# Ternary feed-forward weights made by VectorE instead of GpSimd, and packed weights unpacked later

## The chip, the cores and the metric

The kernel runs on one core of one Trainium2 chip, as one launch of one program. The metric is the device time of that launch in microseconds (us), from its start to the stored output. The core has five engines that run their own instruction streams side by side and meet only at semaphores: TensorE (PE in the profile), VectorE (DVE), ScalarE (ACT), GpSimd (POOL) and SyncE (SP, which here issues every DMA).

## The reference, cut to what matters

Two perceiver layers over 128 query rows of 256 channels, each layer being cross-attention, self-attention and a feed-forward. The two feed-forwards and their weights are what the change is about:

```python
# layer 0's feed-forward: weights rounded to -1, 0, 1 by their own mean magnitude
def _quantize(W):
    gamma = jnp.mean(jnp.abs(W))
    return jnp.clip(jnp.round(W / (gamma + EPS)), -1.0, 1.0)
Wq1, Wq2 = _quantize(W1), _quantize(W2)          # 1024x256 and 256x1024
h = jax.nn.relu(jnp.einsum('bsd,fd->bsf', x, Wq1) + b1)
out = jnp.einsum('bsf,df->bsd', h, Wq2) + b2
# layer 1's feed-forward: four 2-bit weights in each int32
enc = (packed_weight[None, :] >> shifts[:, None] & 3).reshape(-1)[:n]
w = (enc.astype(jnp.float32) - 1.0).reshape(OUT_F, IN_F) * weight_scale
# order of the whole
x = x + _L0_xattn_ref(_layernorm(x), ctx_768, ...)   # 12544 keys
x = x + _L0_attn_ref(_layernorm(x), ...)
x = x + _L0_ffn_ref(_layernorm(x), ...)
x = x + _L1_xattn_ref(_layernorm(x), ctx_768, ..., mask)
x = x + _L1_attn_ref(_layernorm(x), ...)
x = x + _L1_ffn_ref(_layernorm(x), ...)
```

## The kernel before

**Stages.** Layer 0's cross-attention goes over the 12544 keys in 14 chunks of 896 and fills the first 529 us of the span. A short serial stretch follows: its output projection (x0 to x1 in the code's names), the gated self-attention, and the ternary feed-forward. Then comes layer 1's cross-attention over the keys that the mask keeps, its self-attention and its feed-forward. In the serial stretch every step waits for the one before: VectorE normalises `x`, TensorE transposes it, ScalarE copies it out of PSUM, TensorE multiplies, VectorE adds the result to `x`.

**Order.** There is no scheduler. Each engine's stream is written out by hand in its own function, and runs in that order; semaphores (the dictionary `S`) tie the streams together. What an engine has not reached yet is late, however short it is.

**A layernorm needs GpSimd.** `layernorm` (L845 to L859) computes mean and variance on VectorE (L847, L848), adds epsilon (L853, or L851 for the double one), and then asks GpSimd for the power -0.5 through the semaphore `to_power`; GpSimd does it in `power` (L443), and VectorE waits for `power` before it scales `x` into `xn` (L856). The layernorms are tagged x0, x1, x2, x3, x4 and x5. x1, x2 and x3 lie in the serial stretch, and their three calls of `power` stand in GpSimd's stream after the last chunk.

**The ternary weights.** W1 and W2 lie together in the tile `ffw` (128x4096, f32). In the last chunk VectorE sums their magnitudes (L1026), TensorE adds the partitions up (L1499), and VectorE makes of it plus and minus half of the mean, in `thr` (L1034 to L1036). GpSimd then waits for `thr` and turns `ffw` into -1, 0, 1 in four pieces of 1024 columns, with three instructions each: `w < -t` into the scratch tile `wraw` (L508), `w > t` in place (L510), and the difference (L512). The power of x1 stands after the second piece, those of x2 and x3 after the fourth. TensorE waits for all twelve steps (`tern`) before the first product of the feed-forward (L1556); `ffw` is free again when the second (L1563) has ended.

```python
for n in range(4):                                             # GpSimd, from L506
    w, k = ffw[:, 1024 * n:1024 * n + 1024], n // 2
    nc.gpsimd.tensor_scalar(wraw_flat, w, thr[:, 2 + k:3 + k], None, ALU.is_lt ...)
    nc.gpsimd.tensor_scalar(w, w, thr[:, k:k + 1], None, ALU.is_gt ...)
    nc.gpsimd.tensor_tensor(w, w, wraw_flat, ALU.subtract ...)
```

**The packed weights.** `unpack(s)` (two VectorE instructions, L1076 and L1078, on 128x128) is called four times between `thr` and the output of the first attention; its result `wtf` is read by the very last product of the kernel.

**Filling.** Where TensorE would stand idle in the serial stretch, `keep_busy(bank, n)` (L1318) issues n products with a tile of zeros whose result nobody reads. They stand in TensorE's own order, ahead of the wait for the next real operand. Other names used below: L1090 is VectorE's first step on the attention's output; L1109 spreads the logarithm of the gate over 128 columns; L730 is an exponential of ScalarE; L1306 is TensorE's transposition of `xn`; L1539 sums the gates; L1575 makes layer 1's queries; L1151 is VectorE's first step on what they give. At L378 SP waits for the end of the feed-forward (`y` at 3) and then issues the loads of layer 1's first keys.

## Time and profile before

| | us |
|---|---|
| median of 3 runs | 920.91 (920.09 to 921.3) |
| the profiled execution, its own time | 919.66 |
| span of the trace in it | 917.8 |
| TensorE busy | 857.3 |
| VectorE busy | 628.9 |
| ScalarE busy | 427.2 |
| GpSimd busy | 217.6 |

The profile is one execution; its times in the trace count from the start of the span. TensorE is busy for 93% of the span, but part of this is the filling with zeros, so its busy share alone doesn't say that it bounds a stretch. What bounds one is read from the timeline of its engines and from the chain of waits, which follows back from the last instruction what released what. A row of the timeline gives the start, the duration of the (merged) instructions, the engine, line and operation, output and inputs, and in brackets the idle time before it and what ended that.

### The profile page before, as it was taken

How to read it: one execution, taken by the hardware profiler on the slowest of the kernel's cores; microseconds unless marked ns; L12 is line 12 of the kernel's file. 1: busy time of each engine (PE TensorE's matmuls, PEld its weight loads, DVE VectorE, ACT ScalarE, POOL GpSimd, SP SyncE). 2: the span in 40 equal slices, each digit the busy share in tenths (PEclk: the TensorE clock that was granted, in tenths of full speed). 3: DMA queues.
4: the chain of work that ended last, by engine and by line, in shares of the span. 5: the costliest groups of instructions: out<-in, count | busy, mean ns of one | idle time of the engine just before them, and what ended most of it. 6: DMA issues, size and time to landing. Idle time of an engine off the chain costs nothing.

```text
span 917.8 us, 21933 instructions
## 1 busy us (share of the span) xinstructions
PE 857.3 (93%) x7662; PEld 663.3 (72%) x7662; DVE 628.9 (69%) x1104; ACT 427.2 (47%) x578; POOL 217.6 (24%) x233
## 2 busy tenths in 40 slices
PE   3889999999999999999999988998999999999798
PEld 2567777777777777777777757654688887888676
DVE  5768568568568568567567643699487878777373
ACT  2245765765765766766765721300233333333122
POOL 4182022022022022022020392350033232222000
PEclk9669999999999999999999999999999999999798
DMA  5845645645645645648635133210000000000000
GB/s 178 197 128 124 180 114 120 178 115 120 175 118 120 172 120 120 170 123 211 168 85 122 48 139 106 81 39 1 7 19 13 18 14 19 13 19 7 1 1 7
DMA packets 43867, 85.16 MB, mean 93 GB/s; under 512 B 11616, under 2 KB 26657, under 8 KB 41889
## 3 DMA queue, kind: packets, MB, share of 16 engines
q1 hardware_dynamic: 43822, 84.62, 35.9%
q8 instruction: 21, 0.34, 0.2%
q14 instruction: 24, 0.19, 0.1%
HBM read 45.03 MB, written 0.25 MB: 49 GB/s over the span
## 4 chain that ended last, share of the span: by engine, by line
PE 69%; issue 12%; DVE 10%; POOL 4%; ACT 2%; SPq 1%; DMA 1%; DVEq 0%; ACTq 0%; POOLq 0%
PE ps L1642 9%; PE ps L1455 9%; PE ps L1467 8%; PE ps L1373 8%; PE ps L1363 7%; PE ps L1356 6%; DVE cu L918 6%; PE ps L1650 5%; PE ps L1663 5%; PE ps L1643 2%; PE ps L1382 1%; PE ps L1389 1%; POOL ffw L510 1%; POOL wraw L508 1%; PE ps L1616 1%
## 5 line engine op out<-in xcount | busy, mean ns | idle before, releaser
L918 DVE TENSOR_REDUCE cu<-ps 128x1 f32<-128x448 f32 x448 | 250.4, 618 | 53.2 <-PE ps L1373 51.2
L668 ACT ACTIVATE pr<-ps 128x1024 f32<-128x1024 f32 x196 | 190.1, 1023 | 66.4 <-PE ps L1455 65.6
L435 POOL TENSOR_TENSOR pause<-pause 128x1 f32<-128x1 f32 x41 | 12.8, 314 | 569.5 <-DVE mr L930 377.5
L1373 PE MATMUL ps<-khl,qp 32*128 32x448 f32 x448 | 123.9, 483 | 2.6 <-DVE khl L908 0.8
L1455 PE MATMUL ps<-qs,ks 128*128 128x256 f32 x784 | 122.6, 296 | 3.3 <-ACT qs L627 3.1
L1455 PEld LDWEIGHTS ps<-qs,ks 128*128 128x128 f32 x784 | 101.9, 190 | 21.7 <-issue 20.6
L1467 PE MATMUL ps<-pr,v 128*17 128x128 f32 x3136 | 104.6, 274 | 0.5 <-DVE ps L995 0.5
L1642 PE MATMUL ps<-ks,ct 128*128 128x512 f32 x352 | 98.2, 400 | 0.3 <-ACT pr L788 0.3
L1467 PEld LDWEIGHTS ps<-pr,v 128*17 128x17 f32 x3136 | 77.2, 97 | 22.2 <-issue 19.1
L1373 PEld LDWEIGHTS ps<-khl,qp 32*128 32x128 f32 x448 | 57.9, 188 | 48.9 <-DVE cu L918 14.0
L908 DVE SCALAR_TENSOR_TENSOR khl<-ps,bk,khl 128x448 fp32r<-128x448 f32 x56 | 37.1, 682 | 74.5 <-ACT khl L615 74.5
L1206 DVE TENSOR_SCALAR ps<-ps 128x1024 f32<-128x1024 f32 x44 | 54.1, 1229 | 46.2 <-PE ps L1643 46.2
L788 ACT ACTIVATE pr<-ps 128x1024 f32<-128x1024 f32 x44 | 45.3, 1030 | 81.3 <-DVE ps L1206 81.3
L1642 PEld LDWEIGHTS ps<-ks,ct 128*128 128x128 f32 x352 | 64.8, 189 | 17.6 <-issue 3.4
L1363 PE MATMUL ps<-wv,ct 128*128 128x256 f32 x490 | 72.9, 298 | 4.5 <-DVE cu L918 3.6
L1363 PEld LDWEIGHTS ps<-wv,ct 128*128 128x128 f32 x490 | 65.3, 194 | 15.3 <-DVE cu L918 7.9
L1356 PE MATMUL ps<-ct,wk 128*128 128x448 f32 x280 | 68.9, 387 | 2.1 <-DVE khl L908 2.1
L621 ACT COPY v<-ps 128x256 f32<-128x256 f32 x98 | 36.6, 374 | 60.3 <-PE ps L1363 59.1
L1189 DVE TENSOR_TENSOR pr<-pr,wraw 128x1024 f32<-128x1024 f32 x45 | 55.0, 1223 | 4.0 <-issue 4.0
L1356 PEld LDWEIGHTS ps<-ct,wk 128*128 128x128 f32 x280 | 52.5, 198 | 6.4 <-DVE khl L908 2.5
L1193 DVE TENSOR_TENSOR nm<-nm,pr 128x1024 f32<-128x1024 f32 x45 | 55.4, 1232 | 1.5
L1173 DVE CUSTOM_DVE_ANT_0 pr<-ps,khl 128x1024 f32<-128x1024 f32 x48 | 55.5, 1220 | 0.0
(263 smaller groups left out, 1143.7 us busy)
## 6 DMA issues: line engine op xcount, KB each, us to landing
ks<-khl SPq DMA_DIRECT2D x168, 224.0 KB, 4.9
nm<-maxima SPq DMA_DIRECT2D x14, 1024.0 KB, 4.6
raw<-in_ctxT SPq DMA_DIRECT2D x14, 448.0 KB, 3.9
raw<-in_ctxT SPq DMA_DIRECT2D x28, 224.0 KB, 4.4
ffw<-in_mask_q SPq DMA_DIRECT2D x1, 1568.0 KB, 9.6
raw<-in_ctxT SPq DMA_DIRECT2D x12, 128.0 KB, 2.2
raw<-in_ctxT SPq DMA_DIRECT2D x22, 64.0 KB, 1.8
raw<-in_ctxT SPq DMA_DIRECT2D x44, 32.0 KB, 2.0
```

What stands on the lines that cost most here:

```text
L668: nc.scalar.activation(pr[:, (HALVES * b + u) % 4, :], bank(2 * (u % 2), 2), ACT.Exp).then_inc(S["e0_exp"], 1)
L918: V.tensor_reduce(cu2[:, h, half:half + 1], ps[:, use_bank(n), 0:NB], AX_X, ALU.max).then_inc(S["e0_red"], 1)
L1173: nc.vector.tensor_tensor_reduce(out=junk[:, h % 2], in0=ps[:, 2 * (h % 4):2 * (h % 4) + 2, :], in1=negm[:, b, :].bitcast(F32).rearrange(" ...
L1189: V.tensor_tensor(sl, sl, mk[:, u // 2, :].unsqueeze(1).to_broadcast([P, 8, T]), ALU.mult).then_inc(S["e1_masked"], 1)
L1193: V.tensor_tensor(acc, acc, pr[:, u, :], ALU.add).then_inc(S["e1_sum"], 1)
L1206: V.tensor_scalar(bank(2 * (u % 2), 2), bank(2 * (u % 2), 2), 80.0, None, ALU.min).then_inc(S["e1_ok"], 1)
L1356: last = mm(dst, wk0[:, w, t * P:(t + 1) * P], ct[:, b, xx, half * NB:(half + 1) * NB], start=(j == 0), stop=(j == 4))
L1363: last = mm(ps[:, use_bank(n), 0:C], ct[:, b, xx, t * P:(t + 1) * P], wv0[:, w, :], start=(j == 0), stop=(j == 4))
L1373: mm(ps[:, use_bank(n), 0:NB], qp[part, t, e, :], khl[part, 0, t, half * NB:(half + 1) * NB], start=True, stop=True).then_inc(S["e0_head"], 1)
L1455: last = mm(ps[:, 2 * z + k // 2, (k % 2) * 256:(k % 2) * 256 + 256], ks_v[:, b, gg, t * P:(t + 1) * P], qs[:, gg * 256:gg * 256 + 256], s ...
L1467: last = mm(ps[32 * j:32 * j + 17, 4, (h // 4) * T:(h // 4 + 1) * T], v17_v[:, b, t, h, :], pr[:, (HALVES * b + u) % 4, k * T:(k + 1) * T] ...
L1642: mm(ps[:, 2 * z + j, :], cu[:, t, xx, :], asp[:, w, cols], start=(i == 0), stop=False)
```

## The change

GpSimd's twelve instructions and its waits for `thr` and the load of the weights go; its stream goes from the last chunk's work straight to the three powers. VectorE makes the ternary weights, right behind `thr`, with two instructions for each piece: `w < -t` into `wraw`, and one `scalar_tensor_tensor` that takes `(w > t) - wraw` in place. TensorE waits for 4 steps in place of 12. The four calls of `unpack` move from the end of the last chunk to behind the double layernorm x3, ahead of VectorE's wait for layer 1's folded queries.

```diff
@@ GpSimd @@
-            pool.wait_ge(S["thr"], 1)
-            pool.wait_ge(S["ld_ffw"], 32)
             pool.wait_ge(S["e0_lo"], NCH + 1)
-            for n in range(4):
-                w, k = ffw[:, 1024 * n:1024 * n + 1024], n // 2
-                nc.gpsimd.tensor_scalar(wraw_flat, w, thr[:, 2 + k:3 + k], None, ALU.is_lt
-                                        ).then_inc(S["tern"], 1)
-                nc.gpsimd.tensor_scalar(w, w, thr[:, k:k + 1], None, ALU.is_gt).then_inc(S["tern"], 1)
-                pool.wait_ge(S["tern"], 3 * n + 2)
-                nc.gpsimd.tensor_tensor(w, w, wraw_flat, ALU.subtract).then_inc(S["tern"], 1)
-                pool.wait_ge(S["tern"], 3 * n + 3)
-                if n == 1:
-                    power(rstd[:, :], expo[:, 0:1])
-            power(rstd[:, :], expo[:, 0:1])
-            power(rstd[:, :], expo[:, 0:1])
+            for _ in range(3):
+                power(rstd[:, :], expo[:, 0:1])
@@ VectorE @@
             dve.sem_inc(S["thr"], 1)
+            for n in range(4):
+                w, k = ffw[:, 1024 * n:1024 * n + 1024], n // 2
+                link(V.tensor_scalar(wraw_flat, w, thr[:, 2 + k:3 + k], None, ALU.is_lt))
+                V.scalar_tensor_tensor(w, w, thr[:, k:k + 1], wraw_flat, ALU.is_gt, ALU.subtract).then_inc(S["tern"], 1)
+                dve.wait_ge(S["tern"], n + 1)
             dve.wait_ge(S["ld_small"], 16 * 9)
...
-            for n in range(4):
-                unpack(n)
...
             link(V.memset(ml, 0.0))
             link(V.memset(mx[:, :], -3.0e38))
+            for n in range(4):
+                unpack(n)
             total = dve.value_load(sup[0:1, 1, 0:1], min_val=0, max_val=NUNIT)
@@ TensorE @@
-            pe.wait_ge(S["tern"], 12)
+            pe.wait_ge(S["tern"], 4)
```

GpSimd's stream behind the last chunk's work, before (the tile names are those of the code; `rstd` is the layernorm's; a row's `x2` counts two in a row):

```order
L469 TENSOR_TENSOR dm<-con,mr 128x1024
L508 ISA
L508 TENSOR_SCALAR wraw<-ffw,thr 128x1024
L510 TENSOR_SCALAR ffw<-ffw,thr 128x1024
L512 TENSOR_TENSOR ffw<-ffw,wraw 128x1024
```

After, at the same place:

```order
L469 TENSOR_TENSOR dm<-con,mr 128x1024
L443 TENSOR_TENSOR rstd<-rstd,expo 128x1 x3
L508 MEMSET khl 32x256
L511 MEMSET ct 64x2x1024
L515 TENSOR_LOAD sup
```

Of the four triples before, the first is shown; the power of x1 stood behind the second, and now all three powers are next, with nothing of the weights ahead of them.

VectorE's stream behind the thresholds, before:

```order
L1036 TENSOR_SCALAR thr<-thr 128x2
L1037 TENSOR_SCALAR kept<-ps 49x1
L1040 TENSOR_SCALAR con<-con 128x128
L1041 TENSOR_SCALAR slp<-slp 128x16
L1042 TENSOR_SCALAR nbg<-nbg 128x1
L1076 TENSOR_SCALAR wq<-pk 128x128
L1078 TENSOR_SCALAR wq<-wq,fsc 128x2x64
```

After, at the same place (the first of the four pairs):

```order
L1023 TENSOR_SCALAR thr<-thr 128x2
L1024 TENSOR_SCALAR thr<-thr 128x2
L1025 TENSOR_SCALAR kept<-ps 49x1
L1029 TENSOR_SCALAR wraw<-ffw,thr 128x1024
L1030 SCALAR_TENSOR_TENSOR ffw<-ffw,thr,wraw 128x1024
```

The four pairs on 1024 columns have taken the place of the four pairs of `unpack` on 128 (`wq` is the tile under `wtf`), and stand ahead of L1040's counterpart; in both kernels the next instruction behind these is the reciprocal of the attention's output (L1090, L1079 after). In layer 1's beginning VectorE now has:

```order
L1133 MEMSET oacc 128x512
L1134 MEMSET mx 128x16
L1069 TENSOR_SCALAR wq<-pk 128x128
L1071 TENSOR_SCALAR wq<-wq,fsc 128x2x64
L1069 TENSOR_SCALAR wq<-pk 128x128
```

Four such pairs stand there, and behind them the reading of two counts and the step on the folded queries (L1142, which was L1151).

## Rows read from the trace of the kernel before

**Rows 1.** Chain of waits, 529 to 565 us: start, us, engine, output, line

```profile
537.40 2.84 POOL wraw L508
...
553.77 0.57 POOL rstd L443
554.34 0.03 issue
554.37 0.42 DVE xn L856
...
564.50 0.37 SPq L285
```

**Rows 2.** GpSimd's groups by line, 519 to 555 us: busy us, mean ns

```profile
L510 POOL TENSOR_SCALAR ffw<-ffw,thr 128x1024 f32<-128x1024 f32 x4 | 11.7, 2915 | 0.0
L508 POOL TENSOR_SCALAR wraw<-ffw,thr 128x1024 f32<-128x1024 f32 x4 | 11.5, 2868 | 19.6 <-issue 19.4
L512 POOL TENSOR_TENSOR ffw<-ffw,wraw 128x1024 f32<-128x1024 f32 x4 | 9.4, 2354 | 0.3
```

**Rows 3.** VectorE's timeline, x1 to x3: start, us, instruction, idle before it

```profile
535.05 0.15 DVE L853 TENSOR_SCALAR rstd<-mv 128x1 f32<-128x1 f32 x1
537.44 1.21 DVE L856 TENSOR_SCALAR xn<-x,mv,rstd 128x256 f32<-128x256 f32 x1 [2.23 <-POOL rstd L443]
...
543.59 1.99 DVE L1109 TENSOR_SCALAR xn<-con,g 128x128 f32<-128x128 f32 x1 [1.33 <-ACT g L728]
...
550.70 0.15 DVE L853 TENSOR_SCALAR rstd<-mv 128x1 f32<-128x1 f32 x1
...
565.72 0.15 DVE L851 TENSOR_SCALAR rstd<-mv 128x1 f32<-128x1 f32 x1
566.60 0.48 DVE L856 TENSOR_SCALAR xn<-x,mv,rstd 128x256 f32<-128x256 f32 x1 [0.72 <-POOL rstd L443]
```

**Rows 4.** Timeline of TensorE in the serial stretch

```profile
533.88 2.57 PE L1318 MATMUL ps<-zero 128*128 128x256 bf16 x22
538.76 0.44 PE L1306 MATMUL ps<-con,xn 128*128 128x128 f32 x2 [2.31 <-DVEq L862]
...
545.69 0.49 PE L1539 MATMUL ps<-con,xn 128*128 128x128 f32 x2 [1.98 <-DVEq L1110]
...
555.86 5.16 PE L1556 MATMUL ps<-xnT,ffw 128*128 128x128 f32 x32
...
568.60 3.84 PE L1575 MATMUL ps<-xnT,pr 128*128 128x128 f32 x32 [0.41 <-ACT xnT L744]
```

**Rows 5.** Windows: length, busy us of PE, PEld, DVE, ACT, POOL, then granted TensorE clock

```profile
552.00:554.90 2.90, 0.01 (x1) 0.01 (x1) 0.41 (x1) 0.00 (x0) 2.25 (x2) 1.00 0.00 0
554.90:561.00 6.10, 6.10 (x39) 5.81 (x40) 1.12 (x2) 2.26 (x3) 0.00 (x0) 0.72 0.00 0
...
868.00:872.60 4.60, 4.60 (x20) 3.52 (x19) 1.38 (x2) 0.81 (x2) 0.00 (x0) 0.65 0.00 0
```

**Rows 6.** Timeline of VectorE at the kernel's end, forms like the new ones

```profile
888.21 1.23 DVE L1257 SCALAR_TENSOR_TENSOR pr<-pr 128x1024 f32<-128x1024 f32 x1
889.47 0.69 DVE L1260 TENSOR_SCALAR pr<-pr 128x1024 f32<-128x1024 f32 x1
...
911.87 0.35 DVE L1283 TENSOR_SCALAR xn<-xn,rstd 128x256 f32<-128x256 f32 x1
912.26 0.29 DVE L1284 TENSOR_SCALAR xn<-xn 128x256 f32<-128x256 f32 x1
```

**Rows 7.** VectorE's timeline around the thresholds

```profile
519.66 0.15 DVE L1037 TENSOR_SCALAR kept<-ps 49x1 f32<-49x1 f32 x1
519.97 0.23 DVE L1040 TENSOR_SCALAR con<-con 128x128 f32<-128x128 f32 x1
...
530.42 0.26 DVE L1090 RECIPROCAL rl<-ps 128x16 f32<-128x16 f32 x1 [4.45 <-PE ps L1507]
```

**Rows 8.** Timeline of ScalarE: its exponential of the gates

```profile
546.97 0.31 ACT L730 ACTIVATE xn<-xn 128x128 f32<-128x128 f32 x1 [2.11 <-DVEq L1114]
```

**Rows 9.** Timeline of VectorE at layer 1's folded queries

```profile
580.28 2.60 DVE L1151 TENSOR_TENSOR ks<-ps,ks 128x1024 fp32r<-128x1024 f32 x2 [10.01 <-ACT ks L766]
```

## The prediction

> **What bounds the kernel now.** I read the chain of waits first, since it names what released what in the stretch that the change touches. Between the end of the last chunk and the second feed-forward product it runs almost wholly on GpSimd: one of its comparisons starts at 537.40, and its power for the layernorm x2 is done only at 554.34, after which VectorE scales x and the chain goes on to SP's loads for layer 1 at 564.50 [rows 1]. The groups of GpSimd then give the price of this work: four comparisons of 2.87 us, four of 2.92 and four subtractions of 2.35, 32.6 us in all [rows 2]. It begins once the thresholds are there, at about 520, so it can't be over before 553, and the power of x2 is queued behind it.
>
> The timeline of VectorE shows what is waited for. In x3, where GpSimd is free, the step from the start of the epsilon addition to the start of the scaling takes 566.60 - 565.72 = 0.88 us. In x1 it takes 537.44 - 535.05 = 2.39, and in x2 554.37 - 550.70 = 3.67 [rows 1, 3]. TensorE, the engine that is nearly always busy, is idle at just these places: 2.31 us before it can transpose x1, 1.98 before L1539, and for all but 0.01 of the 2.90 us from 552.0 to 554.9 [rows 4, 5]. So here a serial chain is the bound and not an engine's throughput.
>
> **The change part by part.** *The new work on VectorE.* No row shows these instructions, so they are put together from near ones. A comparison of a tensor with a per-partition scalar on 1024 columns: the tensor_scalar on 1024 columns with immediates takes 0.69, and a scalar taken from a tile adds 0.35 - 0.29 = 0.06, so 0.75 [rows 6]. The scalar_tensor_tensor: 1.23 plus the same 0.06, so 1.29 [rows 6]. Consecutive dependent instructions lie about 0.04 us apart in the timeline, and each pair has two such steps. A pair is 2.1 us, and four are 8.5. They start where L1037 has ended and been waited for, at 519.85, and end at 528.4. The three small steps L1040 to L1042 follow, of about 0.2 each with their gaps, so VectorE is through at 529.1 [rows 7]. It next has to be there at 530.42, for L1090, which waits for TensorE [rows 7]. The work is hidden with 1.3 us to spare, by the last chunk's scores, exponentials and weighing, in which VectorE has no part. Cost: 0. From below, it can't be a gain by itself. From above: if the comparison runs no faster than the two-input form, it costs 1.29 too, the pairs end at 530.5, VectorE is through at 531.2 and L1090 starts 0.8 late. I take 0, since L1260 is a row of the same operation, shape and memory.
>
> *Removed from GpSimd.* With 32.6 us gone it is idle when x1 and x2 ask for the power, as it is in x3.
>
> Term A, x1: the wait shrinks by 2.39 - 0.88 = 1.51 [rows 3]. The scaling itself took 1.21 us, with a comparison of GpSimd beside it from 537.40; the same instruction took 0.48 in x3 and 0.42 in x2, where no comparison ran [rows 1, 3]. That is 0.79 more, together 2.30. TensorE has 22 filling products ahead of the transposition, which run from 533.88 to 536.45, and the transposition started at 538.76 [rows 4]. So at most 2.31 can be had here, and the filling is just not late. Term A is 2.3.
>
> Term B, L1109: 1.99 us for 128 columns with one scalar from a tile [rows 3]. L1040 takes 0.23 for 128 columns with immediates [rows 7], plus 0.06 for the scalar is 0.29, so 1.70 goes if GpSimd's presence is the reason, as in x1. Behind it TensorE had been idle for 1.98 and ScalarE's exponential for 2.11 [rows 4, 8], both more than 1.70, so neither filling nor a table load becomes the bound. Term B is 1.7, with 0 as the other end if the length of this instruction has a cause of its own.
>
> *A rule weighed against the row.* The scaling of x1 ran from 537.44 to 538.65, and the comparison beside it from 537.40 to 540.24 [rows 1, 3]: it was held up, but was done 1.6 us before GpSimd was. The Trainium skill (SBUF — State Buffer, section "Who interferes with whom") says of such a pair that the one that issues first has the shared port for its whole instruction and "the other **fully blocks** (not throttle)". By that, the scaling would not have ended before 540.24, and term A could have been 1.6 larger before the filling capped it; by the row it is what stands above. On the direction, that VectorE gains when GpSimd leaves, rule and row agree.
>
> Term C, x2: 3.67 - 0.88 = 2.79 [rows 1, 3]. TensorE's filling doesn't reach into it, since TensorE is idle for 2.9 us before the transposition [rows 5]. Term C is 2.8.
>
> Term D, the clock. After that idle stretch the granted clock of the stretch 554.9 to 561.0 is 0.72: part of the feed-forward's first product runs at 1.2 and not at 2.4 GHz [rows 5]. Its 32 records take 5.16 us, where the 32 records of the same shape in L1575 take 3.84 [rows 4]. With terms A to C the idle stretches of 2.3, 2.0 and 3.1 us shrink to 0.0, 0.3 and 0.3, so I expect no fall here: 1.3, with 0 as the other end.
>
> *TensorE's wait for the weights.* They are ready at 528.4, and needed at about 548: nothing.
>
> *unpack, moved.* Four pairs of about 0.23 and 0.29, some 2.3 us with gaps, come before VectorE's step on the folded queries, in front of which it sat idle for 10.01 us [rows 7, 9]. It issues no DMA and nobody waits on VectorE in there. Cost 0; the cover is ScalarE's and TensorE's making of the queries and the loads of the first keys, and even if it were gone the cost would be 2.3. Taking it from its old place gains nothing, since VectorE waited there for 4.45 us [rows 7].
>
> *What is late next.* Everything behind 564.50 hangs on SP's issue after the feed-forward, and moves forward as a whole. The loads of layer 1's weights are issued at the end of the last chunk and are not in the chain.
>
> **The sum.** 2.3 + 1.7 + 2.8 + 1.3 = 8.1 us. Against the profiled execution's own 919.66 (917.8 of span and 1.9 around it) that gives 911.6. This execution lies 1.25 us under the median of the runs, so for a median I take 920.9 - 8.1 = 912.8.
>
> **The rivals.** *The clock does not follow.* Terms A to C come, but the fall of the clock stays or comes back elsewhere. For it: the trace has falls without an idle stretch before them, as at 868.0 to 872.6, where TensorE is busy for all 4.6 us at 0.65 of the clock [rows 5]. Against it: the fall at 555 comes right after the longest idle stretch of this part. The gain is then 6.8, so 914.1. The Trainium skill (TensorE: Matmul & The Clock Gate, section "What's actually happening") has the chip judge activity in a window that runs freely, so that the point of change differs between runs of one kernel; by that rule any shift of 7 us may move other falls too. How much one is worth is in the row: 0.35 of 4.6 us short of full clock is 1.6 us of work at 2.4 GHz. One more of them with the old one kept makes 915.7, one fewer with the gain of 8.1 makes 911.2.
>
> *VectorE is late for L1090.* The comparison takes 1.29: 0.8 us back, 913.6.
>
> *It was hidden anyway.* If the head of layer 1 waits for something that doesn't move, such as its loads, the gain before 564.50 is lost: 920.9. Against it: SP issues these only after the feed-forward [rows 1].
>
> *Slower.* VectorE may be no better at these comparisons than GpSimd. At 2.9 us for each of the eight, the pairs end at 519.85 + 4 x 5.9 = 543.3, VectorE is through at 544.0 and the attention's output waits 13.6 us for it, in the middle of the chain. Less A to C (6.8), the clock lost, it is 6.8 slower: 927.7. It turns where a pair costs the 2.1 that I expect plus (1.3 + 8.1) / 4 = 2.35 more, at 4.5 us. For it speaks only that no row has a comparison on VectorE; against it that its arithmetic on 1024 columns takes 0.69 to 1.23 throughout [rows 6].
>
> **How the numbers follow.** My forecast 912.8 gets 0.70; the clock that does not follow 0.16 (914.1, up to 915.7); VectorE late 0.06 (913.6); one fall fewer 0.03 (911.2); hidden anyway 0.03; slower 0.02. The range from 911.0 to 915.8 holds the first four, with term B's absence (914.5) too, and leaves out about 1 in 10. A difference under 0.2% (1.8 us) can't be told from no change in a measurement of this kernel. Faster by more: 0.95; within: 0.03; slower: 0.02.
>
> **What would show it.** Right: no GpSimd work between the last chunk and x1; 0.88 us from epsilon to scaling in x1 and x2; 0.42 for the scaling of x1 and 0.29 for L1109; pairs of 0.75 and 1.29; VectorE idle before the reciprocal; granted clock 1.00 through the first feed-forward product, and its 32 records in about 3.85. SP's first load after the feed-forward at about 556.4 in place of 564.5. Wrong: VectorE released by itself at the reciprocal, a clock under 1.00 in the feed-forward, or a gap behind 556 that was not there before.

## The result, and the profile after

| | median, us | lowest to highest |
|---|---|---|
| before, 5 runs | 920.63 | 920.09 to 921.3 |
| after, 5 runs | 907.82 | 906.85 to 913.62 |
| the profiled execution of after | 913.62 | span 911.8 |

The ratio is 0.9877, with a 95% interval from 0.9849 to 0.9905. The changed kernel is faster, by 12.8 us where 8.1 were forecast, and 907.82 lies 3.2 us below the low end of the range.

The two traces are compared first by stage. These are windows of before and then of after: from the start to the end of the second chunk (the opening); the other chunks up to the thresholds; from there to the end of the feed-forward (the serial stretch); layer 1 up to its attention's output; and the tail. A row has the window, its length, the busy time of PE, PEld, DVE, ACT and POOL, and then the granted clock of TensorE, the DMA share and GB/s. The row of the chunks is left out in both.

```profile
0.00:95.23 95.23, 72.98 (x490) 53.30 (x491) 65.54 (x115) 36.41 (x57) 38.23 (x25) 0.84 0.63 160
...
519.06:564.59 45.53, 37.93 (x391) 30.53 (x391) 19.92 (x52) 15.31 (x22) 33.58 (x14) 0.96 0.19 71
564.59:858.88 294.29, 279.87 (x1756) 214.59 (x1756) 225.06 (x299) 78.92 (x81) 74.42 (x146) 0.99 0.10 28
858.88:917.80 58.92, 52.79 (x360) 42.55 (x356) 29.00 (x60) 12.07 (x15) 1.12 (x2) 0.88 0.01 3
```

```profile
0.00:99.32 99.32, 73.44 (x490) 54.00 (x491) 66.39 (x115) 36.41 (x57) 38.03 (x25) 0.86 0.60 154
...
522.96:560.27 37.31, 36.44 (x391) 29.09 (x391) 20.08 (x51) 15.31 (x22) 1.10 (x2) 1.00 0.23 86
560.27:855.59 295.32, 280.96 (x1756) 214.86 (x1756) 226.75 (x306) 78.89 (x81) 75.02 (x146) 0.98 0.10 28
855.59:911.80 56.21, 50.02 (x360) 40.81 (x356) 29.00 (x60) 12.06 (x15) 1.13 (x2) 0.93 0.01 3
```

The serial stretch gave 45.53 - 37.31 = 8.22 us. It is the only stage whose work the change touches, apart from `unpack`. But the opening, whose instructions are the same in both kernels, took 4.09 us more, layer 1's attention 1.03 more, the chunks 0.19 less, and the tail, also the same, 2.71 less. So these two executions lie only 6.0 us apart, and 6.0 is the sum of an 8.2 that belongs to the change and of things that don't. The moved `unpack` is not behind the 1.03 (below); the clock is at 1.2 GHz there from 638.5 to 645.5 us in after (0.51 granted), and for about half as long in before (0.74 from 641.0 to 647.5). The forecast and the miss both sit in this table.

First the stretch itself. VectorE's timeline of after (start, duration, instruction, idle before it and what ended it):

```profile
523.86 0.75 DVE L1029 TENSOR_SCALAR wraw<-ffw,thr 128x1024 f32<-128x1024 f32 x1
524.65 1.28 DVE L1030 SCALAR_TENSOR_TENSOR ffw<-ffw,thr,wraw 128x1024 f32<-128x1024 f32 x1
...
530.97 1.28 DVE L1030 SCALAR_TENSOR_TENSOR ffw<-ffw,thr,wraw 128x1024 f32<-128x1024 f32 x1
...
534.25 0.26 DVE L1079 RECIPROCAL rl<-ps 128x16 f32<-128x16 f32 x1 [1.33 <-PE ps L1498]
...
538.82 0.15 DVE L841 TENSOR_SCALAR rstd<-mv 128x1 f32<-128x1 f32 x1
539.79 0.41 DVE L844 TENSOR_SCALAR xn<-x,mv,rstd 128x256 f32<-128x256 f32 x1 [0.82 <-POOL rstd L443]
...
545.15 0.29 DVE L1098 TENSOR_SCALAR xn<-con,g 128x128 f32<-128x128 f32 x1 [1.33 <-ACT g L716]
...
550.56 0.15 DVE L841 TENSOR_SCALAR rstd<-mv 128x1 f32<-128x1 f32 x1
551.44 0.41 DVE L844 TENSOR_SCALAR xn<-x,mv,rstd 128x256 f32<-128x256 f32 x1 [0.72 <-POOL rstd L443]
```

The four pairs run from 523.86 to 532.25 at 0.75 and 1.28 us each. VectorE then still waits 1.33 us for TensorE before the reciprocal, so the new work is hidden. In x1 the step from epsilon to scaling is 0.97 us and the scaling 0.41; L1098 takes 0.29; in x2 the step is 0.88. The rows that answer to them stand in [rows 3] and [rows 7].

The moved `unpack` stands in layer 1's beginning, ahead of the step on the folded queries:

```profile
575.89 2.60 DVE L1142 TENSOR_TENSOR ks<-ps,ks 128x1024 fp32r<-128x1024 f32 x2 [7.61 <-ACT ks L754]
```

VectorE still waits 7.61 us for ScalarE there (10.01 in before [rows 9]), and the step starts 15.62 us after the stretch's end, where before has 15.69. So the move cost nothing, as forecast.

TensorE's timeline of after, and behind it the window of both feed-forward products:

```profile
537.71 2.57 PE L1309 MATMUL ps<-zero 128*128 128x256 bf16 x22
540.32 0.44 PE L1297 MATMUL ps<-con,xn 128*128 128x128 f32 x2
...
545.55 0.49 PE L1530 MATMUL ps<-con,xn 128*128 128x128 f32 x2 [0.28 <-DVEq L1099]
...
551.97 0.44 PE L1297 MATMUL ps<-con,xn 128*128 128x128 f32 x2 [0.28 <-DVEq L850]
...
552.86 3.84 PE L1547 MATMUL ps<-xnT,ffw 128*128 128x128 f32 x32
```

```profile
552.86:559.99 7.13, 7.13 (x48) 6.63 (x49) 2.57 (x5) 1.84 (x2) 0.00 (x0) 1.00 0.00 0
```

The third idle stretch of before, ahead of x2's transposition, has this row in its timeline of TensorE:

```profile
554.89 0.44 PE L1306 MATMUL ps<-con,xn 128*128 128x128 f32 x2 [3.07 <-DVEq L862]
```

Of the three idle stretches of before (2.31 and 1.98 us [rows 4], and this 3.07) 0, 0.28 and 0.28 are left. The granted clock is 1.00, the level of 2.4 GHz, through both products, and the 32 matmuls take 3.84 us in place of 5.16.

Then the opening. The rows of VectorE and GpSimd in the timeline of before, in order of time:

```profile
13.58 2.63 DVE L893 TENSOR_TENSOR v<-xn,con 128x256 f32<-128x256 f32 x2
13.86 2.08 POOL L457 TENSOR_TENSOR ct<-raw,ct 128x896 fp32r<-128x896 f32 x1 [9.29 <-issue]
...
16.25 2.18 DVE L895 CAST qp<-v 128x512 fp32r<-128x512 f32 x1
...
18.21 6.23 POOL L476 MEMSET ks<- 32x7168 f32 x1
...
19.30 5.17 DVE L901 TENSOR_SCALAR mr<-mx 128x16 fp32r<-128x16 f32 x1
```

And of after, with TensorE's first product behind it:

```profile
13.53 2.07 POOL L457 TENSOR_TENSOR ct<-raw,ct 128x896 fp32r<-128x896 f32 x1 [9.13 <-issue]
13.87 4.22 DVE L881 TENSOR_TENSOR v<-xn,con 128x256 f32<-128x256 f32 x2
...
17.87 6.07 POOL L476 MEMSET ks<- 32x7168 f32 x1
18.13 6.09 DVE L883 CAST qp<-v 128x512 fp32r<-128x512 f32 x1
...
25.26 0.58 PE L1467 MATMUL ps<-zero 128*128 128x512 bf16 x1 [12.07 <-DVEq L885]
```

An instruction of VectorE on 16 columns takes 5.17 us in before: it ends at 24.47, just as GpSimd's memset does at 24.44. In after the memset holds the cast instead: 6.09 us, where the same cast takes 0.43 in `gpsimd_busy` (below), with GpSimd idle beside it. The cast's 2.18 in before is not its own length either, since GpSimd's second subtraction (64x896, from 16.01 to 18.14) runs beside it. The cast stands ahead of TensorE's first product, so TensorE stands for 12.07 us behind it; in before and in `after_ordered` (below) it is 6.58.

The order is made one step earlier. In after GpSimd's first subtraction, on 128x896, starts 0.34 us ahead of VectorE's two products into `v`, and these take 4.22 us; in before it starts 0.28 us behind them, and they take 2.63. Nothing in the program orders these two, so a few tenths of a microsecond decide which instruction is caught. The Trainium skill (SBUF — State Buffer, "Who interferes with whom") has for such pairs the engine that issues first hold the shared port for its whole instruction while the other is blocked; at the memset the traces agree. At x1's scaling they don't: that ended 1.6 us before the comparison beside it [rows 1, 3], as the prediction had it.

### The profile page after: what moved, and what is told of

It is laid out like the page before. It is cut to its first block, busy times and chain, and to the rows that moved or that the text cites. A ratio compares the mean times of both kernels' runs of the same rounds, so it can differ in the third digit from the quotient of the medians.

```text
span 911.8 us, 21931 instructions
## 1 busy us (share of the span) xinstructions
PE 854.5 (94%) x7662; PEld 661.0 (72%) x7662; DVE 631.6 (69%) x1112; ACT 427.1 (47%) x578; POOL 185.5 (20%) x221
## 4 chain that ended last, share of the span: by engine, by line
PE 73%; DVE 11%; issue 11%; ACT 2%; SPq 1%; DMA 1%; DVEq 0%; POOL 0%; ACTq 0%; POOLq 0%
PE ps L1446 10%; PE ps L1633 9%; PE ps L1458 9%; PE ps L1364 8%; PE ps L1354 7%; PE ps L1347 7%; DVE cu L906 6%; PE ps L1641 6%; PE ps L1654 5%; PE ps L1634 2%; PE ps L1373 1%; PE ps L1380 1%; PE ps L1607 1%; PE ps L1309 1%; PE ps L1609 1%
## 5 line engine op out<-in xcount | busy, mean ns | idle before, releaser
L896 DVE SCALAR_TENSOR_TENSOR khl<-ps,bk,khl 128x448 fp32r<-128x448 f32 x56 | 37.3, 684 | 77.2 <-ACT khl L603 77.2
## 6 DMA issues: line engine op xcount, KB each, us to landing
ks<-khl SPq DMA_DIRECT2D x168, 224.0 KB, 5.0
raw<-in_ctxT SPq DMA_DIRECT2D x28, 224.0 KB, 4.3
```

## The experiments

Each kernel ran beside runs of before on the same chip; medians are compared within one session, and kernels of different sessions by their ratios to before. A ratio comes with its 95% interval, and isn't exactly that of the two medians. The expectations on record stand with each. For the stages I use the same five bounds as above; "the stretch" is the serial one.

### The changed kernel again, and both kernels with the opening's order fixed

`after_again` has no edit. `after_ordered` and `before_ordered` are the two kernels with one wait more, which holds GpSimd's first memset of `ks` back until VectorE is through with the opening's steps:

```diff
+            pool.wait_ge(S["v_ones"], 2)
             nc.gpsimd.memset(ks[96:P, 0:GROUPS * CH].bitcast(F32), 1.0)
```

> The changed kernel once more, unaltered. In its first profile the unchanged opening of the kernel was 3.9 us longer than before's (thresholds at 522.96 and not 519.06), while the serial stretch from there to the end of the first feed-forward was 8.2 us shorter (37.31 against 45.53). Theory: the opening can go two ways, according to whether GpSimd's memset of ks (6 us) gets in ahead of VectorE's cast to qp. Where it does, a run takes 912 to 914; where not, 907 to 910. Then the serial stretch is 37.3 +- 0.3 in this profile too, whatever the opening does. Rival: the opening is fixed by the program and the spread comes from TensorE's clock in layer 1; then the thresholds are at 523.0 +- 0.3 again, and the times differ behind the feed-forward.

> The changed kernel, in which GpSimd's first memset of ks waits until VectorE is through with its opening (semaphore v_ones at 2), so that it can't hold up the cast to qp. Theory of the opening: the cast takes 0.4 to 2.2 us and not 6.1, the thresholds come at 519.0 or earlier, and the runs lie together within 1.5 us at 905 to 908. Rival (clock in layer 1): the times still spread over 4 us or more.

> The kernel before, with the same wait in the opening and nothing of the change. It gives the change its value with the opening out of the way. Theory: 917 to 920, and the changed kernel with the same wait is 8 to 10 us faster (8.2 of the serial stretch, the rest from falls of the clock that are met or missed). Rival: the median gain of 12.8 us is all the change's; then the two differ by 12 to 13.5.

| | median, us | runs, lowest to highest | ratio to before | opening | stretch | tail |
|---|---|---|---|---|---|---|
| before, same session | 919.84 | 25, 911.72 to 922.26 | | | | |
| after_again | 910.84 | 8, 909.1 to 914.14 | 0.9922 (0.9892 to 0.9951) | 97.18 | 37.32 | 56.10 |
| after_ordered | 907.59 | 6, 904.48 to 908.81 | 0.9881 (0.9847 to 0.9915) | 92.21 | 37.33 | 59.10 |
| before_ordered | 913.46 | 12, 911.16 to 916.66 | 0.9951 (0.9928 to 0.9975) | 90.59 | 45.32 | 56.69 |

VectorE and GpSimd in the opening of `after_ordered`:

```profile
14.61 2.18 DVE L884 CAST qp<-v 128x512 fp32r<-128x512 f32 x1
16.82 2.44 DVE L885 TENSOR_TENSOR dm<-v,qp 128x512 fp32r<-128x512 f32 x1
19.41 0.17 DVE L890 TENSOR_SCALAR mr<-mx 128x16 fp32r<-128x16 f32 x1
...
20.22 6.07 POOL L477 MEMSET ks<- 32x7168 f32 x1 [1.51 <-DVE v L892]
```

The same instruction on 16 columns takes 0.17 us when the memset is not beside it, and the openings are 95.23 - 90.59 = 4.6 us shorter than in the trace of before above, and 99.32 - 92.21 = 7.1 shorter than in that of after. It holds in every trace: the seven kernels with this wait and no filling in the first chunk (those of this and the next three sections) have openings of 90.59 to 92.21 us, the nine traces without it 93.77 to 99.32. The wait orders only the memset, though: the steps before it still meet GpSimd's two subtractions, here the cast (2.18 for 0.43) and VectorE's own subtraction behind it (2.44 for 0.69, its time in before).

In medians the one wait is worth 919.84 - 913.46 = 6.4 us in before and 910.84 - 907.59 = 3.3 in after. In means of the same runs it is 919.05 - 913.74 = 5.3 and 911.07 - 907.02 = 4.1, each good to some 2 us by the spread of the runs, so both are clear of 0 and can't be told apart. With the order fixed on both sides the change is worth 913.46 - 907.59 = 5.9 us in medians, 6.7 in means (again good to 2), and 45.32 - 37.33 = 8.0 in the stretch.

Three expectations missed. `after_ordered` was to lie within 1.5 us and spread over 4.3, which was its rival's sign (the rest of the kernel varies too); `before_ordered` was to take 917 to 920 and took 913.46; and the two were to differ by 8 to 10. The 25 runs of before also show what three or five close ones had hidden: the unchanged kernel spreads over 10.5 us. No kernel of the study is faster than `after_ordered` beyond the noise.

### Is it GpSimd's absence?

`gpsimd_busy` is `after_ordered` with GpSimd kept busy in the stretch by three triples like the four of before, on scratch data that nobody reads, beginning once VectorE's pairs are done; VectorE's pairs stay. The three powers stand where that work lets them.

```diff
+            pool.wait_ge(S["tern"], 4)
+            spare = raw_flat[:, 0:1024]
-            for _ in range(3):
-                power(rstd[:, :], expo[:, 0:1])
+            for n in range(3):
+                k = (n + 1) // 2
+                nc.gpsimd.tensor_scalar(spare, spare, thr[:, 2 + k:3 + k], None, ALU.is_lt) ...
+                nc.gpsimd.tensor_scalar(spare, spare, thr[:, k:k + 1], None, ALU.is_gt) ...
+                nc.gpsimd.tensor_tensor(spare, spare, spare, ALU.subtract) ...
+                if n == 0:
+                    power(rstd[:, :], expo[:, 0:1])
+            power(rstd[:, :], expo[:, 0:1])
+            power(rstd[:, :], expo[:, 0:1])
```

> The changed kernel with the ordered opening, and with GpSimd given back three triples of the old work (two comparisons and a subtraction on 128x1024) on a tile that nobody reads, begun when VectorE has ended its ternary weights (528.4 by the old clock of the trace) and with the power of x1 behind the first triple and that of x2 behind the third, as they stood. VectorE's new work stays. My steps A to D say that the gain is from GpSimd's absence alone: the steps of x1 and x2 from epsilon to scaling are 2.2 to 2.4 and 3.5 to 3.9 us again, L1098 takes about 2.0, the scaling of x1 1.2, the clock falls in the feed-forward's first product, and the kernel is 7.5 to 8.5 us slower than the one with the ordered opening. Rival: VectorE's own shorter stream or the moved unpacking gives a part; then it is less than 6 us slower.

It took 913.94 us (12 runs, 913.14 to 914.68; ratio 0.9949, 0.9929 to 0.9969), against 907.59 for `after_ordered` and 913.46 for `before_ordered` in the same session. The stretch is 44.63. VectorE's timeline at x1, L1111 (the gate's 128 columns) and x2:

```profile
532.26 1.20 DVE L857 TENSOR_SCALAR xn<-x,mv,rstd 128x256 f32<-128x256 f32 x1 [1.78 <-POOL rstd L443]
...
538.40 1.65 DVE L1111 TENSOR_SCALAR xn<-con,g 128x128 f32<-128x128 f32 x1 [1.33 <-ACT g L729]
...
548.50 0.41 DVE L857 TENSOR_SCALAR xn<-x,mv,rstd 128x256 f32<-128x256 f32 x1 [3.17 <-POOL rstd L443]
```

The same view in the opening, where the cast meets nothing of GpSimd:

```profile
18.77 0.43 DVE L896 CAST qp<-v 128x512 fp32r<-128x512 f32 x1
```

The window at the first feed-forward product:

```profile
549.50:553.50 4.00, 3.98 (x22) 3.68 (x21) 0.00 (x0) 2.26 (x3) 0.00 (x0) 0.57 0.00 0
```

All four terms are back: the wait for the power at x1 and x2, the scaling held up to 1.20, the 128 columns at 1.65, and a clock of 0.57, which is a mix of 1.2 and 2.4 GHz. So the gain is what GpSimd no longer does, and the new work of VectorE costs nothing that can be seen. The whole is smaller than expected (7.5 to 8.5): 44.63 - 37.33 = 7.3 us in the stretch and 6.35 in medians. The stretch lacks 0.7 against `before_ordered`, since the triples don't stand quite where the old ones did: x1 waits 1.78 us for the power and not 2.23 [rows 3], x2 3.17 and not 3.50, and the 128 columns take 1.65 and not 1.99, while the slow clock lies more on the first product, whose 32 records take 5.41 us for 4.60.

### The clock in the feed-forward, by itself

Both start from the ordered kernels, and one number is changed in the filling ahead of x2's transposition. `before_filled` keeps GpSimd's work, and so the wait, but fills it; `after_unfilled` has `keep_busy(6, 1)` at this line: no wait for GpSimd's other work, but next to nothing that fills. The diff is that of `before_filled`, without the opening's wait.

```diff
-            keep_busy(6, 20)
+            keep_busy(6, 45)
             transposes("x2", xn)
```

> The kernel before with the ordered opening, and 45 filling products in place of 20 ahead of the transposition of x2, so that TensorE has no idle stretch of 3.1 us there. GpSimd's work and VectorE's waits stay. Term D of the sum (the clock): the granted clock stays at 1.00 through the feed-forward's first product, its 32 records take 3.85 us and not 5.16, and the serial stretch is 1.2 to 1.5 us shorter than the 45.3 of the ordered kernel before. Rival: the fall has another cause, such as work at half of the rate earlier; then it stays or moves, and the stretch is 45.3 +- 0.3.

> The changed kernel with the ordered opening, and 1 filling product in place of 20 ahead of the transposition of x2, which gives TensorE an idle stretch of 2.5 us there while GpSimd stays idle. The same term from the other side. If idleness of this length makes the fall: 3.4 us at 1.2 GHz behind it, and a serial stretch of 38.5 to 39.0 in place of 37.3. Rival: before x1 an idle stretch of 2.3 us brought no fall in the kernel before; then it is 37.3 +- 0.2.

TensorE in `before_filled`, and then in `after_unfilled` with its window:

```profile
545.92 5.09 PE L1319 MATMUL ps<-zero 128*128 128x256 bf16 x45
551.35 0.44 PE L1307 MATMUL ps<-con,xn 128*128 128x128 f32 x2 [0.34 <-DVEq L863]
...
552.25 3.84 PE L1557 MATMUL ps<-xnT,ffw 128*128 128x128 f32 x32
```

```profile
543.61 0.69 PE L1298 MATMUL ps<-con,xn 128*128 128x128 f32 x2 [2.36 <-DVEq L851]
...
544.94 4.58 PE L1548 MATMUL ps<-xnT,ffw 128*128 128x128 f32 x32
```

```profile
543.00:547.00 4.00, 3.39 (x17) 3.12 (x18) 0.41 (x1) 2.26 (x3) 0.04 (x1) 0.57 0.00 0
```

Filling alone takes the fall away and shortens the stretch of `before_ordered` from 45.32 to 44.12, by 1.2. Taking the filling out brings the fall in and lengthens that of `after_ordered` from 37.33 to 38.50, again by 1.2. In both, what went before the fall is an idle TensorE (3.07 us in before, 2.36 here). Term D is thus 1.2, and belongs to the idle time and not to GpSimd as such.

But an idle stretch isn't enough to forecast a fall: the 2.31 and 1.98 us around x1 in before are followed by none (the clock is 1.00 from 538.8 to 545.7 us), and neither are the same stretches in four kernels with the same code there (`before_copy1`, `before_copy2`, `before_ordered`, `before_filled`), while 2.21 and 1.98 at the same places in `unpack_only` are. What tells them apart isn't shown.

In the medians term D can't be seen: 913.86 for `before_filled` (10 runs, ratio 0.9956, 0.9926 to 0.9985) and 907.10 for `after_unfilled` (4 runs, 0.9887, 0.9819 to 0.9954), against 0.9951 and 0.9881 for the kernels without the edit. An edit of 1.2 us lies inside these intervals, and only the stage shows it. A fall need not cost anything either: in `unpack_only`, below, the clock is 0.51 from 541.5 to 552.0 us, ahead of x2's transposition, and the stretch is no longer for it, since the slow steps used up the time in which the chain otherwise waits for GpSimd's power (0.81 us left of 3.50 at x2).

### The moved unpacking

`unpack_early` is `after_ordered` with the four calls back at the end of the last chunk, now behind VectorE's pairs. `unpack_only` is `before_ordered` with the calls moved as the change does, and GpSimd's work left as it was. The diff is that of `unpack_early`; `unpack_only` is its reverse.

```diff
+            for n in range(4):
+                unpack(n)
             dve.wait_ge(S["o0_q"], 1)
...
             link(V.memset(mx[:, :], -3.0e38))
-            for n in range(4):
-                unpack(n)
```

> The changed kernel with the ordered opening, and the packed weights unpacked in their old place, behind the ternary weights and ahead of the attention's output. My account: VectorE had 1.33 us to spare there in the changed kernel's trace, and the four pairs take 2.35; so the reciprocal starts 1.0 us later, released by VectorE itself, and the serial stretch is 38.2 to 38.4 in place of 37.3. Rival: moving them back is without effect, as the old place had 4.5 us of waiting; then 37.3 +- 0.1.

> The kernel before with the ordered opening and only the second part of the change: the packed weights unpacked in layer 1's beginning, the ternary weights left to GpSimd. My account: no effect, since VectorE waited 4.5 us in the old place and 10 us in the new one; the serial stretch is 45.3 +- 0.2 and the time that of the ordered kernel before, 913.5 +- 1.5. Rival: without VectorE's use of the shared port there, GpSimd's comparisons go faster; then the stretch is 0.3 to 2 us shorter.

VectorE in `unpack_early`, then in `unpack_only`:

```profile
526.88 0.29 DVE L1072 TENSOR_SCALAR wq<-wq,fsc 128x128 f32<-128x128 int32 x1
527.20 0.26 DVE L1083 RECIPROCAL rl<-ps 128x16 f32<-128x16 f32 x1
```

```profile
526.89 0.26 DVE L1089 RECIPROCAL rl<-ps 128x16 f32<-128x16 f32 x1 [9.00 <-PE ps L1508]
```

With both loads in the same place there is no idle time left before the reciprocal. It starts 527.20 - 514.75 = 12.45 us after the thresholds, where after has 534.25 - 522.96 = 11.29, and the stretch is 38.46: 1.1 us more. That is about the 2.3 us of unpacking less the 1.33 that were spare. Moving it alone changes next to nothing: the stretch is 45.09 for 45.32, the reciprocal waits 9.00 us for TensorE, and the ratio is 0.9954 (913.28 us, 10 runs, 0.9922 to 0.9985) beside 0.9951 without the move. So the move is worth nothing in before and 1.1 us once VectorE has the pairs: without it pairs and unpacking together no longer fit into the wait. `unpack_early` ran at 908.44 (10 runs, 0.9907, 0.9881 to 0.9932), which agrees with that and can't be told from 0.

### More executions of the two kernels

`before_copy1`, `before_copy2` and `after_copy1` to `after_copy4` have no edit; each is one execution with its trace, to see how the stages vary. The column before the tail is layer 1 up to its attention's output.

> The kernel before once more, unaltered, for its opening. Its runs have spread from 910 to 922 us. Theory: the opening (up to the end of the second chunk's flag, 95.23 in the first trace) is what differs, with VectorE's 6 us behind GpSimd's memset or without; the stages behind it are within 0.3 us (chunks 423.7, serial 45.3) or within the 3 us of the last stage. So a run at 920 has an opening of 95 to 99, and one at 912 of 90 to 92. Rival: the opening is about 95 in every run, and the spread is in layer 1.

> The same as before_copy1, for a second sample: opening plus 822.6 (the rest of the first trace: chunks 423.8, serial 45.5, folded 15.7, layer 1's attention 278.6, tail 58.9) gives the span within 3 us. Rival as there.

> The changed kernel once more, unaltered. Its serial stretch is 37.3 +- 0.1. Theory: a run at 907 has an opening of 92 to 94, one at 911 to 914 has 96 to 99. Rival: the opening is 97 to 99 each time, and a run at 907 is short in layer 1.

> The same as after_copy1, for another sample of the changed kernel's opening: 92 to 94 in a run at 907, 96 to 99 in one at 911 to 914.

> The changed kernel unaltered, a further sample. So far a trace of a run at 907 to 908, the median of the first comparison, is missing. The serial stretch is 37.3 again; whatever lies outside it (870.1 to 874.5 in the four traces so far, 868.3 to 872.3 in those of the kernel before) has to be 868 to 869 in such a run. Theory: it is the opening that is short there, 92 to 94. Rival: layer 1's two stages, 334.0 at least so far, are at 332.

> The same as after_copy3, one more sample: serial stretch 37.3, opening 92 to 94 in a run at 907 and 96 to 99 in one at 911 to 914.

| trace | time, us | opening | chunks | stretch | layer 1's attention with its queries | tail |
|---|---|---|---|---|---|---|
| before | 919.66 | 95.23 | 423.83 | 45.53 | 294.29 | 58.92 |
| before_copy1 | 915.44 | 93.77 | 423.75 | 45.33 | 294.00 | 56.75 |
| before_copy2 | 915.68 | 94.06 | 423.77 | 45.33 | 294.00 | 56.74 |
| after | 913.62 | 99.32 | 423.64 | 37.31 | 295.32 | 56.21 |
| after_again | 911.54 | 97.18 | 423.69 | 37.32 | 295.41 | 56.10 |
| after_copy1 | 909.24 | 95.66 | 423.77 | 37.31 | 294.52 | 56.14 |
| after_copy2 | 912.27 | 95.84 | 423.83 | 37.33 | 294.50 | 59.00 |
| after_copy3 | 908.58 | 95.49 | 423.50 | 37.33 | 294.40 | 55.98 |
| after_copy4 | 913.67 | 97.44 | 423.60 | 37.31 | 294.36 | 59.09 |

The chunks and the stretch are fixed to 0.3 us. The opening moves by 3.8 us within after alone, the tail by 3.1, layer 1's attention by 1.1. The opening of after has both forms of the collision. In `after`, `after_again`, `after_copy2` and `after_copy4` it is the cast (6.09 us each time). In `after_copy1` and `after_copy3` it is the instruction on 16 columns (5.46 and 5.47), as in all three traces of before (5.17); GpSimd and VectorE in `after_copy3`:

```profile
18.90 6.07 POOL L476 MEMSET ks<- 32x7168 f32 x1
...
19.54 5.47 DVE L889 TENSOR_SCALAR mr<-mx 128x16 fp32r<-128x16 f32 x1
```

In each of the four with the cast caught, GpSimd's subtraction on 128x896 starts 0.02 to 0.39 us ahead of VectorE's products into `v`; in the other five it starts 0.19 to 0.83 behind. The six times of after part the same way: 911.54 to 913.67 with the cast caught, 908.58 and 909.24 without, nearly as the expectation of `after_again` had it. In the opening's length the parting is weaker. The three longest, 97.18 to 99.32, all have the cast caught, but `after_copy2` has it too and takes 95.84, next to 95.66 and 95.49 for the two without; its time is long by its tail. So the collision alone doesn't fix the opening's length. How long the clock is at 1.2 GHz in it varies too, but doesn't go with the length: 27 us in all in `after`, the longest, and 31 in `after_copy1` and `after_copy3`. The tail is 59.0 where a fall of the clock follows the attention's output (at 869 in before, 863.5 in `after_copy4`) and 56 to 56.8 where none does, in both kernels: 2 to 3 us.

### Would a full clock in the opening pay?

The opening of every trace of the two kernels has the clock at 1.2 GHz for 20 to 31 us in all. `after_warm` and `before_warm` are the ordered kernels with three filling products behind each unit of scores of the first chunk, 96 in all, to keep TensorE from standing idle there.

```diff
                 elif kind == "m":
                     unit_scores(c, i, n)
+                    if first:
+                        keep_busy(0, 3)
```

> The changed kernel with the ordered opening, and with three filling products of 256 columns behind each of the 32 score units of the very first chunk, where TensorE has been paced by VectorE's maxima and was granted 1.2 GHz for 17 to 24 us in every trace. Theory: the opening is where runs differ, by who gets the shared port first and by when the clock falls; with both taken away it is 86 to 89 (90.6 to 92.2 with the order alone) and the runs lie within 2 us at 902 to 905. Rival: VectorE alone paces the opening and the clock there costs nothing; then it stays at 90 to 92, and the filling may even cost up to 2 us, since VectorE waits for units behind it.

> The same opening in the kernel before, with nothing of the change. It gives the change's value with the least noise: the two serial stretches differ by 8.0 (45.3 and 37.3) and the medians by 7 to 9. Rival: the first comparison's 12.8 us holds whole; then by 12 to 13.5.

`after_warm` was expected at 902 to 905 us. The two are the slowest kernels of the study: 956.74 us (6 runs, ratio 1.0401, 1.0372 to 1.043) and 966.16 (6 runs, 1.0499, 1.0465 to 1.0534). The clock did what was wanted. Window of `after_ordered`, then of `after_warm`:

```profile
26.00:64.00 38.00, 33.36 (x116) 23.15 (x115) 28.16 (x48) 12.96 (x23) 20.96 (x11) 0.69 0.76 189
```

```profile
26.00:64.00 38.00, 35.66 (x185) 21.17 (x184) 25.43 (x44) 9.33 (x18) 19.00 (x11) 0.96 0.70 165
```

But the opening got longer, 95.49 for 92.21, as its rival had it in kind: the filling stands in TensorE's order ahead of the scores on which VectorE waits, and VectorE did 44 instructions in place of 48 in the same 38 us. And the chunks behind it, in which nothing was changed, took 469.75 us in place of 423.64. From the timeline of TensorE and from the page's part on DMA queues (packets, MB, share) of `after_warm`; behind them that line of `after_ordered`:

```profile
216.17 2.23 PE L1348 MATMUL ps<-ct,wk 128*128 128x448 f32 x5 [7.00 <-issue]
...
q8 instruction: 67, 1.10, 0.5%
```

```profile
q8 instruction: 21, 0.34, 0.2%
```

TensorE's chunks are a loop of six turns over two chunks each. At the five returns to its top TensorE waits 35.1 us in all for nothing that the trace shows ("issue"), 6.7 to 7.3 each time, and every second chunk takes 43.2 to 44.4 us in place of 34.5. The queue that brings instructions moves 46 packets and 0.76 MB more. `before_warm` has the same: 6.8 to 7.6 us at each return, chunks of 470.04. The reading that fits is that the loop's instructions are fetched anew at each return, while they were still at hand without the 96 matmuls ahead of the loop. The Trainium skill (Runtime: NRT & Kernel Launch, "Instruction fetch mechanics") states that a taken branch to code outside the window held on the chip has to fetch it before going on; packets and waits agree with it. Why 96 instructions ahead of the loop should matter, when the loop itself is the same, was not tried and stays open. The pair still gives the change's worth once more: 9.4 us in medians (7 to 9 expected), 45.75 - 37.33 = 8.4 in the stretch.

## Why the prediction was right, and where it was wrong

**The stretch, by its terms.** All of it held.

| | forecast, us | measured, us |
|---|---|---|
| pairs on VectorE | 0.75 and 1.29, cost 0 | 0.75 and 1.28, reciprocal waits 1.33 |
| A, x1: wait and scaling | 2.3 | (2.39 - 0.97) + (1.21 - 0.41) = 2.2 |
| B, the 128 columns | 1.7 | 1.99 - 0.29 = 1.7 |
| C, x2's wait | 2.8 | 3.67 - 0.88 = 2.8 |
| D, the clock | 1.3 | 5.16 - 3.84 = 1.3; 1.2 by either filling experiment |
| unpacking moved | 0 | 0 in its new place, 0 moved alone; it saves 1.1 beside the pairs |
| sum | 8.1 | 8.2 in the profiled pair, 8.0 to 8.4 in the others |

The 1.3 us to spare came out as 1.33, and in the chain of waits SP's first load after the feed-forward is at 560.19, 37.2 us after the thresholds where before had 45.4 ([rows 1], 564.50 - 519.06). Term A's 0.1 less is GpSimd's start, 0.09 us later than in x2. The filling at x1 was just not late, as forecast: it ends at 540.28, and the transposition starts at 540.32.

**The rivals.** The clock did follow, and VectorE was not late. It was not hidden, and not slower. "One fall fewer" came true in the profiled execution's tail (58.92 to 56.21), at 2.7 us where I had priced it at 1.6. But that was luck and not the change: two of three traces of before have the short tail, and two of six of after the long one. And what the runs showed in place of a single fall with a chance of 0.03 is that three untouched stages move by 1 to 4 us each from trace to trace.

**The number.** What failed is the last step of "The sum", on which "How the numbers follow" rests: "so for a median I take 920.9 - 8.1". It takes everything outside the stretch as fixed, save for a fall of the clock with 0.03 of a chance. The traces show the rest of the span (span less stretch) between 868.3 and 872.3 in the three traces of before, and between 869.4 and 874.5 in the six of after, from the opening and the tail. The three runs shown lay within 1.2 us of one another, and I read that as the spread of the kernel; 66 runs of before in all sessions go from 910.41 to 924.23 with a median of 919.85. The 17 runs of after go from 906.85 to 914.14 with a median of 910.44, so their medians, pooled over sessions, lie 9.4 us apart. In the one later session with several runs of both it is 919.84 - 910.84 = 9.0, and 7.2 by its ratio (interval 4.5 to 9.9, where that of the first comparison gives 8.7 to 13.9). That is closer to the 8.2 of the stretch than the 12.8 of the first comparison, so most of what the first comparison had beyond the forecast fits chance in which executions were drawn; 910.44 still lies just under my range, whose 4.8 us were narrow for a kernel that spreads over 14.

The sign of what was missing could have been read beforehand: before's opening holds an instruction on 16 columns that takes 5.17 us, a collision that nothing in the program orders. A stage with such a row can't be carried over as a constant, in either direction.

**What stays open.** A run of after at 907.8 needs 907.8 - 1.9 - 37.3 = 868.6 us outside the stretch. Traces of before reach 868.3, but the lowest of after is 869.4, at 908.58. No trace was caught at the 907 of the first comparison, nor one of before above 919.66. So the 4.6 us beyond the stretch fit the spread of the unchanged stages in size, but which stage gave them in those runs isn't shown. The cast was caught in four traces of six of after and in none of three of before; whether the change tilts that race or it is chance isn't shown. The medians of the ordered kernels differ by 5.9 us and their stretches by 8.0, which the spread of the runs allows; no stage was found that takes the 2.1 back.

## What to carry to other kernels

When work leaves an engine that a serial chain calls for short steps, count the steps: each one's queueing, the slowing of its neighbours, and the clock that falls in the gap. Added up row by row, that sum held to 0.1 us in the stretch. Before putting it on a median, ask what else the time consists of: look in every stage, also the untouched ones, for rows far longer than their shape (16 columns in 5.17 us), and widen the range by what they could become. And when a race between two engines costs microseconds, one wait that settles it may be worth a good part of the change under study (here 4 to 5 us beside 8).

## What the runs showed of the hardware

- A memset of GpSimd that only writes (32x7168, 6.07 us) held VectorE's cast (6.09 for 0.43 us) and a tensor_scalar on 16 columns (5.17 to 5.47 for 0.17 us) until it had ended. A tensor_tensor of GpSimd did the same: the cast took 2.18 us beside the one on 64x896, ending at 18.43 where that one did at 18.14 (before).
- A GpSimd comparison held VectorE only in part (1.20 us for 0.41, done 1.6 us before the comparison), while L1111 beside the subtraction in `gpsimd_busy` ended at 540.05, just when the subtraction did at 539.97, and its counterpart L1109 in before at 545.58, the subtraction at 545.49.
- A scalar taken from a tile instead of an immediate adds 0.05 to 0.06 us to a tensor_scalar or scalar_tensor_tensor on 1024 columns: 0.75 and 1.28, against 0.69 and 1.23 [rows 6].
- 96 matmuls ahead of a loop made each of its five returns cost 6.7 to 7.6 us of waiting in both kernels, and 46 us in all with the lower clock behind it (0.74 from 216.5 to 224.0 us in `after_warm`); why is open.
